# Alternating the halves of a product with the banks of the scores in a two-layer graph attention kernel

## The reference

```
proj   = x @ W                      # W is 256 x 512
Wh, Ws = split(proj, 2)
scores = Wh @ Ws.T                  # 4096 x 4096
a      = softmax(scores) * adj      # adj is a 4096 x 4096 input
out    = leaky_relu(a @ Wh + x, 0.01)
```

## Time and profile before

| | |
|---|---|
| profiled execution: its own time | 1591.92 us |
| its span, first to last instruction | 1590.1 us |
| timed runs | 1590.1 and 1595.33 us |
| PE matmuls busy | 1552.6 us, 98% |
| DVE busy | 1345.5 us, 85% |
| POOL busy | 802.9 us, 50% |
| ACT busy | 645.4 us, 41% |
| mean granted TensorE clock | 0.998 of full speed |

### The profile page before, as it was taken

The page is one execution under the profiler, slowest core; times in us unless marked ns, Lnnn a source line. Parts: engine busy times, 40 slices in busy tenths (PEclk is TensorE's granted clock), DMA queues, the critical chain, the costliest instruction groups (busy, mean ns, idle before and its releaser), DMA issues. The chain is left out here.

```text
span 1590.1 us, 23354 instructions
## 1 busy us (share of the span) xinstructions
PE 1552.6 (98%) x8104; PEld 1315.7 (83%) x8104; DVE 1345.5 (85%) x1577; ACT 645.4 (41%) x1177; POOL 802.9 (50%) x799
## 2 busy tenths in 40 slices
PE   8999999999999999999799999999999999999996
PEld 7888888888888888888687888888888888888885
DVE  5778877887887788788847899999999999999998
ACT  5344344444444344444433444443444444334432
POOL 0155555555555555555412555555555555555555
PEclk9999999999999999999999999999999999999999
DMA  5377777776777777777924777777777877787775
GB/s 166 116 190 202 184 201 191 193 200 190 193 193 198 187 198 195 195 199 209 256 79 127 197 192 213 191 200 190 205 203 197 207 198 203 186 208 193 202 217 147
DMA packets 166981, 302.57 MB, mean 190 GB/s; under 512 B 39760, under 2 KB 67408, under 8 KB 166736
## 3 DMA queue, kind: packets, MB, share of 16 engines
q1 hardware_dynamic: 104800, 131.84, 33.0%
q0 software_dynamic: 37200, 135.28, 30.1%
q10 hardware_dynamic: 24864, 33.98, 8.0%
HBM read 157.29 MB, written 9.44 MB: 105 GB/s over the span
## 5 line engine op out<-in xcount | busy, mean ns | idle before, releaser
L1223 POOL TENSOR_TENSOR a_lo<-turned,a_hi 128x512 fp32r<-128x512 f32 x488 | 629.8, 1305 | 623.8 <-ACT a_hi L831 621.9
L659 PE MATMUL banks<-wh,a_hi 128*128 128x512 f32 x1952 | 699.9, 398 | 13.8 <-POOL a_lo L1223 13.8
L799 ACT ACTIVATE ring<-banks,neg_max 128x1024 f32<-128x1024 f32 x256 | 286.1, 1117 | 862.0 <-DVE neg_max L979 848.2
L661 PE MATMUL banks<-wh,a_lo 128*128 128x256 f32 x1952 | 548.1, 281 | 0.0
L659 PEld LDWEIGHTS banks<-wh,a_hi 128*128 128x128 f32 x1952 | 367.4, 188 | 105.3 <-POOL a_lo L1223 11.8
L979 DVE TENSOR_REDUCE neg_max<-banks 128x1 f32<-128x1024 f32 x256 | 312.0, 1219 | 156.6 <-PE banks L544 156.5
L542 PE MATMUL banks<-x_t,q_t 128*128 128x512 f32 x1024 | 406.9, 397 | 2.5 <-DVE q_t L943 1.8
L544 PE MATMUL banks<-x_t,q_t 128*128 128x512 f32 x1024 | 402.4, 393 | 0.0
L543 PE MATMUL banks<-x_t,q_t 128*128 128x512 f32 x1024 | 400.3, 391 | 0.0
L661 PEld LDWEIGHTS banks<-wh,a_lo 128*128 128x128 f32 x1952 | 368.9, 189 | 7.9
L1019 DVE SCALAR_TENSOR_TENSOR ring<-ring,weight,load 128x1024 f32<-128x1024 f32 x251 | 326.3, 1300 | 0.6 <-DMA load<-adj 0.4
(11 more groups left out here) (97 smaller groups left out, 892.4 us busy)
## 6 DMA issues: line engine op xcount, KB each, us to landing
load<-adj POOLq DMA_DIRECT2D x254, 512.0 KB, 5.2
turned<-ring SPq DMA_DIRECT2D x1500, 64.0 KB, 4.1
turned<-ring ACTq DMA_DIRECT2D x500, 64.0 KB, 3.3
rows<-x SPq DMA_DIRECT2D x32, 128.0 KB, 3.3
x_scratch<-rows SPq DMA_DIRECT2D x32, 128.0 KB, 3.1
rows<-x_scratch SPq DMA_DIRECT2D x30, 128.0 KB, 3.6
first_rows<-x SPq DMA_DIRECT2D x30, 128.0 KB, 3.1
out<-rows SPq DMA_DIRECT2D x30, 128.0 KB, 3.2
```

The source lines that it names most:

```text
L659: nc.tensor.matmul(psum[:, bank, :], of_hi[:, b], wh[:, k].rearrange("p a d -> p (a d)"), start=start, stop=stop, skip_group_check=True)
L661: last = nc.tensor.matmul(psum[:, bank, 0:D], of_lo[:, b], wh[:, k, 0], start=False, stop=stop, skip_group_check=True)
L799: nc.scalar.activation(ring_at(i).rearrange("p (r b j) -> p b r j", r=2, j=QUAD), psum[:, 2 * (i % 2):2 * (i % 2) + 2, :].rearrange("p h ( ...
L1223: nc.gpsimd.tensor_tensor(operand(1, j).rearrange("p b (r j) -> p b r j", r=QUADS), as_f32(turned_in[unit_place(unit)][:, :, b:b + SUB, :] ...
```

## The change

PE: `scores` takes a half of a product and makes it between its first and its second bank; the second half follows where the whole product stood. ACT: in step s it makes the high part of half 2k + 1 first, then starts its transfers, and then, ahead of the exponential of step s, makes the high part of half 2k + 2, that is the first half of the next step. The order on DVE, POOL and SP is the same as before. The first product of a layer and the last four steps keep the old order on PE.

```diff
-            def scores(i):
+            def scores(i, between=None):
...
                     last = three_products(psum[:, 2 * (i % 2) + b, :],
                                           [(q[:, 0, kt], q[:, 1, kt], bank_nodes(0, kt, c, b), bank_nodes(1, kt, c, b))
                                            for kt in range(KT)])
+                    if b == 0 and between is not None:
+                        product(between)
                 last.then_inc(scores_done, 1)
...
-                scores(chunk_at(step))
+                k = product_at(step)
+                halves = k is not None and k % CHUNKS > 0
+                scores(chunk_at(step), 2 * k if halves else None)
...
-                if product_at(step) is not None:
-                    product_of_chunk(product_at(step))
+                if halves:
+                    product(2 * k + 1)
+                elif k is not None:
+                    product_of_chunk(k)
...
                 k, summed = product_at(step), tile_at(step - CPT)
+                follows = product_at(step + 1)
                 if k is not None:
-                    split_a(2 * k)
+                    split_a(2 * k + 1)
                 if summed is not None:
                     chunk_factors(summed)
-                if k is not None:
-                    split_a(2 * k + 1)
                 if weighed_at(step) is not None:
                     move_blocks(weighed_at(step))
...
                     split_side(side)
+                if follows is not None:
+
+                    split_a(2 * follows)
                 exponentials(chunk_at(step))
```

## The result

The changed kernel takes 1666.79 us (two runs, 1664.01 and 1669.57), against 1592.71: the ratio is 1.046, with a 95% interval from 1.044 to 1.048. The forecast was 1633, and its range ended at 1665. The direction and the kind of wait were right and the count of waits was not: 74 us where I had summed up 40.

What follows compares the result with a forecast made beforehand. PE, never waiting in 83% of the span, was taken as the bound. Lost ties of 32 and 7 us plus 1.4 us at layer ends made 40 us on 1591.9: 1632, or 1633 against the median; range 1590 to 1665.

Steps and rivals of the forecast that it cites:

- the stretches: 84.7 to 742.3 and 872.0 to 1529.6 us: PE never waits there, 83% of the span, so nothing to win.
- The new wait on first halves: Even steps: the first half's low part, behind ACT's transfers, ends about 6.6; PE wants it at 6.99, 0.4 us left.
- weighing and low part exclude each other: DVE's L1019 and POOL's L1223 now meet; one waits until the other has ended, 0.92 or 0.94 us more in one case.
- so I count one loss of 1.15 us in eight steps, 28 times: Both layers: one PE wait per eight steps, 32 us; second ties lost in perhaps one of five add 7 us.
- the run of eight: Eight steps followed through turn, transfers, high and low part: a tie in step 2, loss there or step 4, step 6 hidden.
- Landings: Step 1: SP's fifth transfer takes 4.0 us, landing at 3.4, later about 3.6; so ACT decides, unless a landing is late.
- ACT's transfers: Three in even steps take 2.03 us, in places 1.80 or 2.06; step 0 was reckoned with 1.80.
- The high part behind one transfer: Step 1: turn ends at 3.33, one transfer follows, and the high part starts at 3.93.
- End of a layer: DVE enters the last steps 1.41 us late; 1.4 us for both layers, bounds 0 and 2.8.
- Rival 1: Contention stays off PE: low part wins the ties, DVE hides L1019's lateness in its idle time; 1588 to 1596 us, chance 0.30.
- Rival 2: DVE becomes the bound in the second layer, a step 0.5 us too long, 58 us; time 1670, chance 0.10.
- Rival 3: The clock falls after a PE wait, losing 1.6 us each, 28 times, 44 us more; time 1677, chance 0.05.

Runs made afterwards that it cites:

- act_alone: ScalarE's new order with PE's old one (both banks, then both halves), on the changed kernel; 1591.83 us, ratio 0.999.
- pe_alone: PE's new order with ScalarE's old one (both high parts behind the exponential), on the changed kernel; 2011.03 us, one run.
- adj_quarter: The changed kernel with each load of adj fetching only the first 256 of its 1024 columns; 1641.07 us, one run.
- adj_quarter_six: The changed kernel reading a quarter of adj, with SP starting six and ACT two transfers of an odd chunk (five and three before); 1591.23 us, one run.
- sp_six: The changed kernel with all of adj, SP starting six and ACT two transfers of an odd chunk (five and three before); 1626.61 us, ratio 1.020.

## Why the prediction was wrong, by its own steps

**Right.** That the stretches had nothing to win. The maximum at 4.39 (measured 282.94 - 278.57 = 4.37). The new wait on first halves alone; none of the 64 waits is in a second half. That weighing and low part exclude each other: in step 0 above, the low part started at 5.30 (5.29 forecast) and the weighing took 2.14 (2.10). The size of a loss, 1.15 us, was 1.06. `act_alone` and `pe_alone` came out at the numbers that this picture gives.

**The step that failed: "so I count one loss of 1.15 us in eight steps, 28 times".** It was 64 times, and the count was the term of the sum that was mis-sized: 68 us of waits instead of 32 to 39. Three inputs of the run of eight were too small:

- *Landings.* "4.0 to landing make 3.4 of this step, with the later turn about 3.6; so ACT decides". The median landing of odd chunks is 4.2 to 5.0 us of a step in the first layer. It is SP's fifth transfer that lands last, in all 114 odd chunks of the two stretches; it takes 4.6 us (median) where the forecast had 4.0 and the same transfer took 3.9 and 3.7 before. I took the duration from a kernel in which ACT had started its three 1.2 us ahead of SP's five; after the change all eight start together, behind the same turn. ACT's three then take 5.0 instead of 3.3 us, but they are down first. That starting together is what makes them slow is argued, not shown. With most of adj's bytes gone (`adj_quarter`), the 18 waits behind odd steps fell to 1 and the time by 26 us.
- *ACT's transfers.* I used the 1.80 us of one row for step 0 and called the next step a tie "decided by 0.04 us". Rows of 2.03 and 2.06 stood beside it. The median of the 114 even steps of the changed kernel is 2.06, and of the 28 with remainder 0 only 3 are near 1.80; the run shown above, at 270.14, is one of these, and its turn in step 2 is late because the high part of step 1 waited for the landing. With 2.06 and landings in time (`adj_quarter`), a low part that still comes first in step 0 moves the end of the turn of step 2 to 3.14 instead of 2.67, and there the low part is mostly 0.2 to 0.5 late. `adj_quarter_six`, 0.6 us shorter there, has one wait, `adj_quarter` 45. Step 0 itself, which the forecast had as safe at 5.29 against 5.53, is the tie with 2.06 (5.56 against 5.51).
- *The high part behind one transfer.* I let it start at once; it starts 0.19 us later (273.62 to 273.81 above).

Since every quantity of the run feeds the next step through the turn, errors of 0.2 to 0.7 us were enough to double a count. A chain whose outcome I had called a tie deserved an upper bound of more than two losses in eight: of the 28 groups of eight steps, the step with remainder 0 lost in 11, that with 2 in 16 and that with 4 in 19.

**End of a layer.** I took 1.4 us; the stage between the stretches and the end grew by 1.7 and 4.7. DVE's later entry does not explain the larger one: `pe_alone` and `sp_six` have PE's new order too, and their last stages take 61.8 us each, 1.3 more than the 60.5 before. The other 3.4 us of the changed kernel's 65.2 stay open.

**Rivals.** Rival 1 (DVE hides it) would need the low part to come first, or early enough, in every step that PE depends on; of the runs with PE's new order and POOL making it, that came about only in `adj_quarter_six`, and there DVE did hide it. Rival 2 (DVE becomes the bound) did not happen: DVE is busy 591 of 694 us in the second layer, less than the 615 before, though the weighing grew: L1066 (now L1075), one of the small instructions of the rows, has a mean of 525 instead of 1400 ns in the first stretch. That these no longer meet POOL is the likely reason. Rival 3 (the clock) did not happen: 1.00 in the stretches in spite of 64 waits of about 1 us, and the passage between banks was free in `pe_alone`. The Trainium skill, in "TensorE: Matmul & The Clock Gate", section "A second HAM failure mode: psum-queue depth-cycling", tells of a kernel that goes round the banks, has small idles between its groups, and sees the clock swing. Here the passages bring no idle (pieces of 1.39 to 1.46 us), and the clock stays; what such idles would do, no run here shows.

**The range** ended at 1665, 72 us above the median, on the bound of two losses in eight (64 us) and with nothing for the landings, which I had named as a sign of error but not priced. That the measured time is only 1.8 us beyond it says little for the sum: the count of waits was more than twice the one I took.

## What to carry to other kernels

A matmul engine that never waits gains nothing from a new order, but a new order can move two other engines onto the same moment. When phases move by 1.4 us, list which pairs of instructions on DVE and POOL now overlap, and price a collision by the slack behind it, not by its length: with a mean weighing of 1606 ns `adj_quarter_six` has one wait, with 1552 the changed kernel has 64. Take the duration of a transfer as valid only for the traffic around it: SP's medians ran from 2.5 to 4.4 us in these runs. And when a repeating chain comes out as a tie, treat the count of losses as unknown up to every step.

## What the runs showed of the hardware

- Who holds the other: in the changed kernel the low part kept its 1.27 to 1.30 us in all cases where it started before the weighing or with it; where it started 0.03 to 0.08 us after, either of the two was held (24 cases); from 0.1 us on a weighing that nothing had held before kept its 1.27 in 60 of 61 cases. The one that was held ended 1.07 to 1.16 us after the other. The Trainium skill ("SBUF — State Buffer", "SBUF: two separate sides") gives the shared ports to whoever starts first. From 0.1 us on the trace agrees; the rows 481.96 and 482.01 above show the second by 0.05 us winning.
- A step of the alternating order without a wait is 5.57 us instead of 5.59: 655.5 against 657.6 us for the first stretch. That is 0.3%, which no version with all of adj could keep. 655.5 is from one run, with a quarter of adj.
